# Attention of an audio tower in twelve steps a batch: weighing in 32-column groups, other places for five pieces of work

## What is computed

```python
h = tokenizer(x)                            # conv, mean of pairs, layer norm
a = _layernorm(h)
q = a @ W_q; latent = (a @ W_k + a @ W_v) @ W_down_kv
k = latent @ W_up_k; v = latent @ W_up_v    # 16 heads of 16
scores = einsum('bhqd,bhkd->bhqk', q, k) / sqrt(256) * exp(-0.01 * |i - j|)
h = h + (softmax(scores) @ v) @ W_o
h = h + mixture_of_16_experts(_layernorm(h)) + shared_ffn(_layernorm(h))
```

## Time and profile before

| | |
|---|---|
| runs shown | 2008.25, 2015.07, 2016.47 us (median 2015.07) |
| profiled execution | 2018.32 us |
| its span | 2016.4 us, mean granted TensorE clock 0.932 |
| busy, share of span | PE 87%, VectorE 61%, ScalarE 46%, GpSimd 47% |
| chain that ended last | PE 70%, VectorE 10%, issue 8%, GpSimd 6%, ScalarE 3% |
| L1483 weighing | 1536 matmul records, 167.6 us busy, mean 358 ns |
| L1742, L1759 experts | 493.7 and 256.6 us busy |

### The profile page before, as it was taken

The page is one execution under the profiler, slowest core; times in us unless marked ns, Lnnn a source line. Parts: engine busy times, 40 slices in busy tenths (PEclk is TensorE's granted clock), DMA queues, the critical chain, the costliest instruction groups (busy, mean ns, idle before and its releaser), DMA issues.

```text
span 2016.4 us, 46453 instructions
## 1 busy us (share of the span) xinstructions
PE 1751.3 (87%) x14894; PEld 1327.7 (66%) x14894; DVE 1232.4 (61%) x3822; ACT 934.9 (46%) x2157; POOL 947.8 (47%) x945
## 2 busy tenths in 40 slices
PE   6857887887888878785899995999999999999997
PEld 5855665665666666563677773777777777777775
DVE  3884666666666666674767866555555555555551
ACT  3535555444554545452533254444444444444442
POOL 3852333333332333324622323466666666666665
PEclk9987888889987988898999996999999999999999
DMA  5524444444443434442321104243443344443322
GB/s 179 187 77 88 102 103 98 97 93 93 97 98 88 101 93 98 100 96 68 105 51 32 30 27 159 84 114 98 102 109 94 101 111 97 99 97 98 94 31 29
DMA packets 220234, 187.39 MB, mean 93 GB/s; under 512 B 165624, under 2 KB 200952, under 8 KB 214008
## 3 DMA queue, kind: packets, MB, share of 16 engines
q1 hardware_dynamic: 193272, 141.99, 26.0%
q0 software_dynamic: 26880, 44.36, 11.0%
HBM read 135.37 MB, written 50.44 MB: 92 GB/s over the span
## 4 chain that ended last, share of the span: by engine, by line
PE 70%; DVE 10%; issue 8%; POOL 6%; ACT 3%; DMA 2%; DVEq 1%; SPq 1%; POOLq 0%; ACTq 0%
PE psum L1742 24%; PE psum L1759 12%; PE psum L1483 6%; PE psum L1607 6%; PE psum L1493 4%; PE psum L1627 4%; PE psum L1467 2%; PE psum L1516 2%; PE psum L1455 2%; DVE psum L1136 2%; ACT arena L756 2%; PE psum L1504 2%; PE psum L1441 2%; POOL arena L612 1%; DVE arena L1127 1%
## 5 line engine op out<-in xcount | busy, mean ns | idle before, releaser
L1742 PE MATMUL psum<-arena,hidden 128*128 128x376 f16 x3072 | 493.7, 323 | 1.1 <-DVE arena L1362 0.9
L655 POOL TENSOR_TENSOR arena<-arena 128x376 f16<-128x376 f32 x320 | 319.7, 1001 | 353.7 <-ACT arena L756 352.3
L1742 PEld LDWEIGHTS psum<-arena,hidden 128*128 128x128 f16 x3072 | 301.1, 98 | 189.5 <-issue 1.9
L1136 DVE TENSOR_TENSOR psum<-psum,constants 128x376 f32<-128x376 f32 x384 | 212.9, 555 | 218.7 <-PE psum L1467 218.5
L756 ACT ACTIVATE arena<-arena 128x376 f16<-128x376 f32 (+5 forms) x610 | 283.6, 473 | 58.8 <-DVE arena L1298 46.6
L805 ACT ACTIVATE arena<-psum 128x376 f32<-128x376 f32 x384 | 184.9, 482 | 232.5 <-PE psum L1455 227.0
L971 ACT ACTIVATE arena<-psum 128x376 f32<-128x376 f32 x256 | 123.9, 484 | 342.7 <-PE psum L1742 342.7
L756 ACT ACTIVATE arena<-psum 128x376 f32<-128x376 f32 (+7 forms) x457 | 167.6, 398 | 228.5 <-PE psum L1483 123.5
L1127 DVE CUSTOM_DVE_ANT_0 arena<-psum,constants 128x188 f32<-128x188 f32 x768 | 237.6, 347 | 41.2 <-PE psum L1441 36.0
L1372 DVE SCALAR_TENSOR_TENSOR arena<-psum,arena 128x376 f32<-128x376 f32 x256 | 140.8, 550 | 189.9 <-ACT arena L971 188.5
L1759 PE MATMUL psum<-hidden,arena 128*128 128x256 f16 (+1 forms) x2304 | 256.6, 273 | 0.0
(11 more groups left out here) (158 smaller groups left out, 2801.2 us busy)
## 6 DMA issues: line engine op xcount, KB each, us to landing
arena<-q_halves SPq DMA_DIRECT2D x384, 47.0 KB, 2.1
arena<-k_halves SPq DMA_DIRECT2D x384, 47.0 KB, 2.1
arena<-e_g SPq DMA_DIRECT2D x16, 1024.0 KB
arena<-e_u SPq DMA_DIRECT2D x16, 1024.0 KB, 5.1
arena<-e_d SPq DMA_DIRECT2D x16, 1024.0 KB
arena<-x_t SPq DMA_DIRECT2D x32, 376.0 KB, 3.5
weighed<-arena POOLq DMA_DIRECT2D x32, 376.0 KB, 3.3
q_halves<-arena SPq DMA_DIRECT2D x32, 188.0 KB, 3.1
```

What stands on the lines that cost most here:

```text
L655: nc.gpsimd.tensor_tensor(dst, f, hi, ALU.subtract).then_inc(ready, 1)
L1136: nc.vector.tensor_tensor(TB[i % 3], TB[i % 3], C[:, at:at + 2 * S], ALU.mult).then_inc(multiplied, 1)
L1742: last = mm(bank[2 * (s % 2) + i][:, 0:CHUNK], w_, a, start=n == 0, stop=n == 5)
```

## The change

- `weigh`: V gets 32 columns a pair and tile. A quarter is four groups of 32 PSUM partitions, one per head: first the head's own tile over 128 rows (tile 0 for head 0, tile 2 for head 1), then its 64 rows of tile 1. Eight matmuls in place of six. The copies of the values (`values`) write the same elements.
- The first half of the values is projected in step 9, into the upper half of bank 5, whose lower part holds the weighed sums; ScalarE copies it in step 11, and the second half in step 2. `weigh` of the last quarter waits for that copy.
- GpSimd's order in a round: low half of the input, heads out, division of b-2, low half of the heads of b-2, low half of the queries, dense heads, low half of the keys. Two waits are added on transfers of the round before (`od_in` on GpSimd, `rd_in` on SyncE).
- ScalarE copies the weighed heads after its job in steps 1, 4 and 7; the high half of the maxima moves from step 10 to 8, the normalized input from 8 to 9.
- TensorE turns the maxima in step 7 (was 9). VectorE: low half of the maxima in 9 (was 11), adding the output in 10 (was 9), statistics in 11, moments and their copy in step 0 of the next round.
- Halves by head parity: the columns of two weights are permuted on the host, so a half holds the heads of one parity. The dense side of each read is two transfers of long rows (8 x 188 elements) in place of six; the block side keeps six. The read of the key blocks goes ahead of the inverse sums on SyncE.
- Rounds 2 and 3 are written out, and one more closing round.

```diff
-            for b in range(-4, 2):
+            for b in range(-4, 4):
...
-            for b in range(B - 4, B + 2):
+            for b in range(B - 4, B + 3):
...
+            def read(blocks, dense, dram, c, single, par, landed):
+                both = 1 - single // 2
+                if blocks is None:
+                    for low, r, n in ((1, single, 1), (0, both, 2)):
+                        src = dram[c, low, :, :, :].rearrange("h (d a) n -> (h d) (a n)", a=HP)
+                        sp.dma_start(dense[par][32 * r:32 * (r + n), :], src.unsqueeze(0).broadcast_to((n, 32, HP * S)) if n > 1 else src).then_inc(landed[par], 16)
...
+                    read(KD, None, k_dram, b + 1, 2, 1 - par, st_in)
                 c = b - 1
                 if valid(c):
                     sp.wait_ge(sums_inverse, c + 1)
                     hold(sp)
+                    at_least(sp, rd_in, 64 * c)
+                    hold(sp)
                     sp.dma_start(r_dram[:, :].rearrange("h (q n) -> (h q) n", q=4), RS[0:64, :]).then_inc(rs_out, 16)
-                if valid(b + 1):
-                    read(KD, None, k_dram, b + 1, (0, 0, 1), 1 - par, st_in)
...
             def batch(b, par):
+                low(XTL[1 - par], XF, XTH[1 - par], xth_ready, b + 3, xtl_ready)
+                heads_out(b - 1, 1 - par)
+                divide(b - 2)
                 low(OTL, ON, OTH, oth_ready, b - 2, otl_ready)
-                heads_out(b - 1, 1 - par)
-                low(XTL[1 - par], XF, XTH[1 - par], xth_ready, b + 3, xtl_ready)
+                low(QS[:, 2 * S:4 * S], QF, QS[:, 0:2 * S], qh_ready, b + 3, ql_ready)
                 dense_heads(b - 1)
-                low(QS[:, 2 * S:4 * S], QF, QS[:, 0:2 * S], qh_ready, b + 3, ql_ready)
                 low(KS2[:, 2 * S:4 * S], KF, KS2[:, 0:2 * S], kh_ready, b + 3, kl_ready)
-                divide(b - 1)
...
-                    if n == 1:
-                        keep_heads(b - 1, 1 - par, 3)
-                    elif n % 3 == 1:
-                        keep_heads(b, par, (n - 4) // 3)
...
                         high(XTH[1 - par], XF, b + 3, xf_ready, xth_ready)
-                        evacuate_values(b + 1)
-                    elif n in (2, 3):
-                        values(b + 1, 1 - par, n - 2)
+                        keep_heads(b - 1, 1 - par, 3)
+                    elif n == 2:
+                        evacuate_values(b + 1, 1)
+                        values(b + 1, 1 - par, 0)
+                    elif n == 3:
+                        values(b + 1, 1 - par, 1)
...
                     elif n == 8:
+                        high_max(b + 1, 1 - par)
+                    elif n == 9:
                         x_norm(b + 4)
                     elif n == 10:
-                        high_max(b + 1, 1 - par)
+                        keep_heads(b, par, 2)
+                    elif n == 11:
+                        evacuate_values(b + 2, 0)
...
+                if g == 3 and valid(c + 2):
+                    pe.wait_ge(vf_ready, 2 * c + 5)
                 pe.wait_ge(exp_done, NS * c + 3 * g + 3)
-                for t in range(3):
-                    for u in range(2):
-                        v = (t * HP + 2 * g + u) * 64
-                        p = (6 * g + 3 * u + t) % NS * S
-                        last = mm(OB[64 * u:64 * u + 64, :], V[cpar][:, v:v + 64], PT[:, p:p + S], start=t == 0, stop=t == 2)
+                for n in range(2):
+                    for k in range(4):
+                        a, h2 = 2 * g + k // 2, k % 2
+                        t, p0, rows = ((0, 0, 128), (2, 0, 128))[h2] if n == 0 else (1, 64 * h2, 64)
+                        v, p = (t * HP + a) * 32, (3 * a + t) % NS * S
+                        last = mm(OB[32 * k:32 * k + 32, :], V[cpar][p0:p0 + rows, v:v + 32], PT[p0:p0 + rows, p:p + S],
+                                  start=n == 0, stop=n == 1)
...
-                if n == 9 and valid(b + 1):
+                if n == 7 and valid(b + 1):
...
-                if n == 11 and valid(b + 2):
+                if n == 9 and valid(b + 2):
                     pe.wait_ge(xtl_ready, b + 3)
-                    if valid(b - 2):
-                        pe.wait_ge(y_added, b - 1)
-                    else:
-                        pe.wait_ge(kf_ready, b + 4)
+                    if valid(b + 1):
+                        pe.wait_ge(vf_ready, 2 * b + 4)
+                    if valid(b):
+                        pe.wait_ge(os_ready, 4 * b + 2)
                     project_values(b + 2, par, 0)
...
+    by_pair = np.arange(D).reshape(HP, 2, HD).transpose(1, 2, 0).reshape(D)
```

More of the change, by code:

```diff
@@ L189, in build @@
         MT = [at2(HS, F16) for _ in range(2)]
-        V = [at2(3 * HP * 64) for _ in range(2)]
+        V = [at2(3 * HP * 32) for _ in range(2)]
         at3 = Place()
@@ L283, in build @@
         TB = [bank[2 + i][:, 0:2 * S] for i in range(3)]
-        OB, XB, WB = bank[5][:, 0:S], bank[6], bank[7]
+        OB, VB, XB, WB = bank[5][:, 0:S], bank[5][:, D:2 * D], bank[6], bank[7]
         def valid(b):
@@ L308, in batches @@
         def batches(eng, body):
-            for b in range(-4, 2):
+            for b in range(-4, 4):
                 body(b, b % 2)
-            with nc.Fori(1, B // 2 - 2, engines=bass.OrderedEngineSet([eng.engine]), head_slot={eng.engine: 0}) as i:
+            with nc.Fori(2, B // 2 - 2, engines=bass.OrderedEngineSet([eng.engine]), head_slot={eng.engine: 0}) as i:
                 body(2 * i, 0)
                 body(2 * i + 1, 1)
-            for b in range(B - 4, B + 2):
+            for b in range(B - 4, B + 3):
                 body(b, b % 2)
@@ L463, in _ @@
             meet(sp)
[L465 to L473, removed]
-                        else:
-                            dst = dense[par][p:p + HD, :].rearrange("p (a n) -> p a n", n=S)
-                        sp.dma_start(dst, rows(dram, c, h2, lows[r])).then_inc(landed[par], 16)
+            def read(blocks, dense, dram, c, single, par, landed):
[4 more added lines that the diff above has]
+                        sp.dma_start(dense[par][32 * r:32 * (r + n), :], src.unsqueeze(0).broadcast_to((n, 32, HP * S)) if n > 1 else src).then_inc(landed[par], 16)
+                else:
+                    for h2 in range(2):
+                        for r in range(3):
+                            p = 32 * r + HD * h2
+                            sp.dma_start(blocks[par][p:p + HD, :].rearrange("p (a n) -> p a n", n=CW)[:, :, h2 * HS:h2 * HS + S],
+                                         dram[c, int(r == single), h2, :, :].rearrange("(d a) n -> d a n", a=HP)).then_inc(landed[par], 16)
             def write(dram, c, halves, low_ready, landed):
@@ L492, in spread_halves @@
                     hold(sp)
[L493 removed]
+                    read(QD, None, q_dram, c, 0, par, s_in)
                     sp.wait_ge(k_out, 16 * c + 16)
                     hold(sp)
[L496 removed]
+                    read(None, KX, k_dram, c, 2, par, s_in)
                 if valid(b + 1):
@@ L499, in spread_halves @@
                     hold(sp)
-                    read(None, QX, q_dram, b + 1, (0, 1, 0), 1 - par, st_in)
+                    read(None, QX, q_dram, b + 1, 0, 1 - par, st_in)
+                    read(KD, None, k_dram, b + 1, 2, 1 - par, st_in)
                 c = b - 1
@@ L617, in heads_out @@
                     hold(pool)
+                    at_least(pool, od_in, 32 * c)
+                    hold(pool)
                     nc.gpsimd.dma_start(SUMS[0:64, :], OS[par][HD:128:32, :].rearrange("j (g q n) -> j g q n", g=4, q=4)).then_inc(sums_in, 16)
@@ L844, in values @@
                     at_least(act, weighed, 4 * c - 4)
[L845 to L853, removed]
+                for t, p0, n, q0, at in (((0, 0, 128, 0, 0), (1, 0, TAIL, 0, D)), ((1, 64, 64, 0, 0), (2, 0, 64, 64, 0), (2, 64, TAIL, 0, D)))[h2]:
+                    src = VF[q0:q0 + n, at:at + D].rearrange("p (a h d) -> p a h d", h=2, d=HD)[:, :, h2, :]
+                    dst = V[par][p0:p0 + n, :].rearrange("p (t a w) -> p t a w", t=3, w=32)[:, t, :, 0:HD]
+                    copy(dst, src).then_inc(v_ready, 1)
             def high_max(c, par):
@@ L1497, in project_values @@
             def project_values(c, par, t):
-                rows = (128, TAIL)[t]
+                rows, to = ((128, VB), (TAIL, WB[0:TAIL, D:2 * D]))[t]
                 n = 0
@@ L1503, in project_values @@
                     for a, w_ in split3(XTH[par][:, x], XTL[par][:, x], WH[:, w], WL[:, w]):
-                        last = mm(WB[0:rows, t * D:(t + 1) * D], a, w_, start=n == 0, stop=n == 5)
+                        last = mm(to, a, w_, start=n == 0, stop=n == 5)
                         n += 1
-                if t == 1:
-                    last.then_inc(v_done, 1)
+                last.then_inc(v_done, 1)
             def project_out(c):
@@ L1795, in score_tables @@
```

(7 more changed lines are left out.)

65 lines of the change are left out of this document (37 added, 28 removed).

## The result

The changed kernel takes 2043.0 us (median of four) against 2013.2 before: ratio 1.015, interval 1.012 to 1.017, so 30 us slower. Forecast were 1826, a range of 1806 to 1880, and faster. The profiled execution has a span of 2042.2 us.

A forecast was written before the change was run, and what follows sets the result against it. No engine full; TensorE's waits for GpSimd and VectorE and a low clock bind. Twenty-six rounds save 180 us, earlier ones 11, closing 2: 193 off, 1822 against the median, plus 4 for jitter: 1826 us, range 1806 to 1880.

The forecast's parts named there:

- the part on halves by head parity: Weight columns permuted on the host, dense reads in two transfers of long rows: no engine does more, nothing in the sum.
- The cover named for the new waits: New waits on GpSimd and SyncE cost nothing, covered by 5 us that SyncE has over in a round of 17.
- Rival 4: Reads through memory close their own loop, or weighing goes one by one, eating the gain: 2015 to 2025 us, chance 0.02.
- The two waits go: TensorE's once-a-round waits, for GpSimd before the query projection (2.1 us) and VectorE before the input's turn (2.0), nearly vanish.
- Rounds of 17.3 by the two rules: TensorE and VectorE pace each other through maximum, turned scores and decay product; attention rounds fall from 24.23 to 17.3 us.
- Weighing in fours: Weighing matmuls in 32-column groups run four at once on TensorE: 0.80 us a weighing, 0.31 less.
- rival 2: Weighing groups run in pairs or partly: 0.63 us more per weighing, 2.2 a round, up to 1885 us, chance 0.10.
- rival 3: Weight loads stop the weighing matmul before them: 3.9 us a weighing, 2160 us, slower than before, chance 0.04.
- Clock: TensorE's granted clock in the attention rounds rises above 0.97, from 0.89.
- Division one batch on, at cost nothing: GpSimd divides batch b-2 instead of b-1, so its 126.8 us wait for the inverse sums goes; added waits cost nothing.

The follow-up runs named there:

- a_split: The changed kernel with each dense read's transfer of two copies (64 rows) split into two transfers of 32 rows: 1850.6 us, ratio 0.9195 to before.
- d_oldreads: The changed kernel with the reads and column order of the kernel before, six transfers on each side: 1853.1 us, ratio 0.9207 to before.
- turn9: a_split with the maxima turned in step 9 again and their low half in step 11: 1878.2 us, ratio 0.934 to before.
- xlow_late: a_split with the input's low half behind the two head transfers on GpSimd again: 1940.2 us, ratio 0.964 to before.
- c_parity_split: The kernel before with only the parity halves and the new reads, their two-copy transfer split into two of 32 rows: 2013.7 us, ratio 1.000.

## Why the prediction was wrong

**The step that failed** is the part on halves by head parity: "reads of the dense side take two transfers of long rows. No engine does more." Only SyncE's issues were counted (24 to 16, 3.8 us less, "of which none is on the path"), and the change of the reads stood in the sum at nothing. Not looked at was over how many DMA engines a transfer is divided. In its place the runs showed a transfer that holds the DMA engines at a share of 0.12, with the sums behind it landing in 7.4 us instead of 2.1. The edit of `a_split` alone gives back 192 of the 217 us between forecast and result. The pattern stood in the diff: a `broadcast_to` with the copies outermost. The cover named for the new waits, "the 5 us that SyncE has over", was never tested against issues that take two and a half times as long (6.97 us against 2.83), and even without the long transfer SyncE saves nothing (11.0 us a round against 11.1, d_oldreads).

**Rival 4** named the place, reads through memory closing a loop of their own, with a chance of 0.02 and a time of 2015 to 2025, still 18 us short of what was measured. It had no cause to make it likely; the cause was in the diff. The loop, as program order and the waits above put it: sums to VectorE's inverse (7.4 us), inverse out (5.8), sums in and key write, key read onto the two engines, the scores of step 6, which let the next round's heads go.

**The rest held in kind.** Without that transfer 1850.6 were measured, inside the range of 1806 to 1880 and 25 over the forecast. Point by point:

- *The two waits go:* shown, and by turn9 and xlow_late each comes back with its piece of work.
- *Rounds of 17.3 by the two rules:* 18.30 on average in a_split; a size missed by 1.0 a round, which is the 25 us. From one inverse (L1098) to the next the first three rounds take 19.0, 23.2 and 19.3, nearly all later ones 17.8 to 18.8, most of them 17.8 or 17.9. Worked through without rounding, the rules give 17.2 with weighing at 0.80 and 17.5 at the 0.91 measured. TensorE's 90 waits for VectorE's decay product, 40.0 us, are in the rules; what makes the last 0.4 of a common round, and the long ones at the start, no run here shows.
- *Weighing in fours:* right in kind. In a_split sixteen records pass in 0.91, from 502.69 to the next turned scores at 503.60:

```profile
502.69 0.98 PE L1493 MATMUL psum<-arena 128*32 128x188 f32 x16
503.60 0.34 PE L1474 MATMUL psum<-arena 96*128 96x188 f16 x2
```

  That is 0.11 more than the four turns and the ends. The loads come in two bursts of eight, at 502.69 and 503.14, so each half takes 0.45: two turns of 0.16 and 0.14 besides, where the forecast had 0.17 for the whole. In pairs (rival 2) it would have been 1.43, with loads that stop the matmuls (rival 3) 3.9. The gain was 12 us for the kernel, not the 26 that 0.31 less on three steps of 28 rounds makes.
- *Clock:* 0.99 in the attention rounds of a_split, above 0.97 as forecast.
- *Division one batch on, at cost nothing:* with the old place 1854.6 were measured, no difference that can be told; it gives nothing either.

## What to carry to other kernels

Read in every new transfer which dimension is outermost and how large it is. Two copies outermost cost 192 us here, and each copy in a transfer of its own nothing (c_parity_split); copies on an inner dimension were not tried. A slow transfer is charged to whoever stands behind it on the same DMA engines, so price it by what queues there (here sums of 11.8 KB for VectorE) and not by its own reader alone. Fewer transfers are not less work for the queue that issues them: measure what one issue of the new shape takes (eighteen took 11.0 us, twenty-four 11.1). Slack on queues hides such a loss (15 us in the old order) until a tighter schedule needs it (192 us): a denser order and a longer transfer are not to be costed apart.

## What the runs showed of the hardware that I had not expected

Two transfers a round, each of 64 rows of 3008 bytes with the two copies outermost, left the sixteen DMA engines at a share of 0.12 for some two microseconds, and a transfer of 11.8 KB from another engine's queue landed in 7.4 us in place of 2.4. Six block reads whose issues took 2.69 us in the old layout (d_oldreads) took 3.87 in the new one (a_split). A wait put back on TensorE cost half its length in one case (28 us for 1.9 a round) and more than its length in another (90 us for 2.3 each time). In the first TensorE's waits for VectorE shrank in return (38.3 to 6.9 us) and in the second they did not (34.9); in both the granted clock fell (0.99 to 0.94 and 0.93) and made TensorE's own work longer, by 0.7 and 1.2 us a round.
